# Summing the weighted values of every second early pair on TensorE instead of VectorE

## The reference

```python
q = x @ Wq + bq
kv = (x @ Wdown + bdown) @ Wup + bup
k, v = split(kv.reshape(B, T, 16, 16), 2, axis=-1)     # 16 heads of 8 each
att = softmax(einsum('bthd,btgd->bthg', q, k) / sqrt(8), axis=-1)   # g: 16 heads of the same token
out = einsum('bthg,btgd->bthd', att, v).reshape(B, T, 128) @ Wout + bout
...
x = x + attention(xn) + experts0(xn)       # 8 experts, 2 per token
x = x + long_convolution(xn) + experts1(xn)
```

## Time and profile before

| | |
|---|---|
| three runs | 1330.55, 1329.0, 1339.67 us; median 1330.55 |
| the profiled execution | 1335.22 us, of which 1333.3 us are the span of the trace |
| busy in the span | PE 1042.1, PEld 879.2, DVE 739.9, ACT 583.7, POOL 803.9 us |
| DVE in L1187, all 32 pairs | 141.0 us, 4406 ns each |
| PE in L838 (sums of scores), 11 pairs | 105.4 us, 767 ns a record |

### The profile page before, as it was taken

How to read it: one execution, slowest core, us unless ns; L and a number is a source line. 1 busy time by engine, 2 the same in 40 slices (tenths; PEclk the granted TensorE clock), 3 DMA queues, 4 the chain that set the end, 5 groups by cost and what they waited for, 6 DMA issues and landing times. The chain is left out here.

```text
span 1333.3 us, 19064 instructions
## 1 busy us (share of the span) xinstructions
PE 1042.1 (78%) x6498; PEld 879.2 (66%) x6498; DVE 739.9 (55%) x953; ACT 583.7 (44%) x1518; POOL 803.9 (60%) x669
## 2 busy tenths in 40 slices
PE   5553776788988898888714678898879999999995
PEld 4521333367777777777613577888868888888884
DVE  7755988998888898888697643211122200000007
ACT  1200111166676777767503673000006666666651
POOL 4065675568888888888875136566544544444444
PEclk9876886799999999999856888998979999999998
DMA  9912322335554555555281021698966867666649
GB/s 294 355 47 102 120 84 109 108 93 151 155 162 139 154 170 149 161 150 159 68 325 57 1 84 44 197 279 252 296 196 195 270 193 196 194 190 196 199 135 356
DMA packets 120245, 226.03 MB, mean 170 GB/s; under 512 B 16961, under 2 KB 80405, under 8 KB 118102
## 3 DMA queue, kind: packets, MB, share of 16 engines
q1 hardware_dynamic: 102164, 188.45, 46.1%
q0 software_dynamic: 17600, 35.71, 7.3%
q10 hardware_dynamic: 386, 0.66, 0.2%
HBM read 157.33 MB, written 67.42 MB: 169 GB/s over the span
## 5 line engine op out<-in xcount | busy, mean ns | idle before, releaser
L498 POOL DMA_INDIRECT y_tok<-FF,yidx x284 | 283.3, 997 | 205.9 <-ACT FF L586 142.6
L490 POOL DMA_INDIRECT sorted_x<-XN,idx x256 | 247.9, 968 | 140.1 <-issue 88.0
L810 PE MATMUL ps<-FF 128*128 128x128 f32 x2272 | 285.8, 280 | 0.0
L810 PEld LDWEIGHTS ps<-FF 128*128 128x128 f32 x2272 | 274.0, 197 | 15.6 <-issue 4.8
L797 PE MATMUL ps<-FF 128*128 128x256 f32 x1136 | 272.3, 383 | 0.0
L576 ACT ACTIVATE FF<-ps,FF 128x256 f32<-128x256 f32 x568 | 231.4, 473 | 36.8 <-PE ps L797 29.1
L797 PEld LDWEIGHTS ps<-FF 128*128 128x128 f32 x1136 | 206.9, 192 | 22.7
L294 POOL TENSOR_TENSOR BG<-TPB 128x2048 f32<-128x2048 f32 x42 | 188.8, 4519 | 30.0 <-ACT TPB L603 20.8
L838 PE MATMUL ps<-BG,cst 128*128 128x512 f32 x176 | 105.4, 767 | 57.8 <-DVE BG L1144 40.5
L1176 DVE TENSOR_TENSOR BG<-ps,TPB 128x1024 f32<-128x1024 f32 x128 | 147.3, 1212 | 0.0
L1187 DVE TENSOR_REDUCE BG<-BG 128x256 f32<-128x4096 f32 x32 | 141.0, 4406 | 0.0
(11 more groups left out here) (203 smaller groups left out, 1462.0 us busy)
## 6 DMA issues: line engine op xcount, KB each, us to landing
FF<-in_moe SPq DMA_DIRECT2D x142, 514.0 KB
TPB<-in_kpad SPq DMA_DIRECT2D x22, 1024.0 KB
sorted_x<-TPB SPq DMA_DIRECT2D x36, 520.0 KB, 5.4
FF<-sorted_x SPq DMA_DIRECT2D x142, 130.0 KB
BG<-y_tok SPq DMA_DIRECT2D x12, 1024.0 KB, 9.2
FF<-in_kpad SPq DMA_DIRECT2D x10, 1024.0 KB
y_tok<-FF,yidx POOLq DMA_INDIRECT x284
xt_d<-BG SPq DMA_DIRECT2D x16, 256.0 KB, 4.4
```

The source lines that it names most:

```text
L490: pool.indirect_dma_start(sorted_x[layer], bass.IndirectOffsetOnAxis(ap=idx[:, k, j:j + 1], axis=0), XN[:, j, :], None).then_inc(s_sc, 16)
L498: pool.indirect_dma_start(y_d[layer], bass.IndirectOffsetOnAxis(ap=yidx[:, G % 4, r:r + 1], axis=0), ys[:, G % 4, r * D:(r + 1) * D], None ...
L810: t = pe.matmul(psY[:, r * P:(r + 1) * P], hT[:, G % 2, m, r * P:(r + 1) * P], wc[:, G % 4, HID + m * D:HID + (m + 1) * D], start=False, s ...
```

## The change

For the pairs 0, 2, 4, 6 and 8 (`BY_PE`) the sum over the 16 products moves from DVE to PE. The layout follows: ACT writes those values with the head ahead of the channel, and the weights with the query's head innermost; DVE's four products are written as 16 slices of 256 (tile, channel, query head); PE adds the slices by 16 matmuls with the identity into `psH[1]`, at the start of its step m+2 (`sum_values`); DVE scales them from PSUM in its step m+2, between `scores` and `weighted` (`by_sums`). As `psH[1]` is needed for that, the queries of all early pairs lie in `psH[0]`: `evac_qkv(m)` waits for the product of pair m-1, where it waited for that of pair m-2, and the evacuation of pair 1 moves behind the exponential of the routing. PE's step 10 waits, ahead of its first expert tile, for the scaling of pair 8.

```diff
+BY_PE = (0, 2, 4, 6, 8)
...
 def evac_qkv(m, t):
                 if m < OWN:
                     if t == 0:
-                        wait(act, s_own, m - 1)
-                    for dst, c in ((psH[m % 2][:, t * D:(t + 1) * D], 0), (qkv[:, m % 4, t, D:2 * D], D)):
+                        wait(act, s_own, m)
+                    for dst, c in ((psH[0][:, t * D:(t + 1) * D], 0), (qkv[:, m % 4, t, D:2 * D], D)):
...
-                    act.copy(qkv[:, m % 4, t, 2 * D:3 * D], bank[:, 2 * D:3 * D]).then_inc(s_qkv, 1)
+                    v, w = qkv[:, m % 4, t, 2 * D:3 * D], bank[:, 2 * D:3 * D]
+                    if m in BY_PE:
+                        v, w = v.rearrange("p (g e) -> p g e", e=DH), w.rearrange("p (e g) -> p g e", e=DH)
+                    act.copy(v, w).then_inc(s_qkv, 1)
...
 def pair_exp(b):
-                act.activation(psP[:, :], S[:, b % 2, :], ACT.Exp, scale=SCALE).then_inc(s_exp, 1)
+                if b in BY_PE:
+                    w = psP[:, :].rearrange("p (t g h) -> p t h g", t=2, g=H)
+                else:
+                    w = psP[:, :].rearrange("p (t h g) -> p t h g", t=2, g=H)
+                act.activation(w, S[:, b % 2, :].rearrange("p (t h g) -> p t h g", t=2, g=H), ACT.Exp, scale=SCALE)\
+                    .then_inc(s_exp, 1)
...
-            for m in range(2):
-                for t in range(2):
-                    evac_qkv(m, t)
+            for t in range(2):
+                evac_qkv(0, t)
             act.wait_ge(s_rin, 1)
             act.activation(best[:, 4, :], best[:, 4, :], ACT.Exp).then_inc(s_ex, 1)
+            for t in range(2):
+                evac_qkv(1, t)
...
+            def sum_values(m):
+                pe.wait_ge(s_pv, m + 1)
+                wait(pe, s_on, m - 1)
+                for g in range(H):
+                    t = pe.matmul(psH[1][:, 0:2 * D], ident, prodv[:, g * 2 * D:(g + 1) * 2 * D],
+                                  start=(g == 0), stop=(g == H - 1))
+                t.then_inc(s_vs, 1)
...
             for b in range(LAST_STEP + 1):
                 tiles = tiles_of(b)
+                if b - 2 in BY_PE:
+                    sum_values(b - 2)
                 if b == T_FIRST:
                     pe.wait_ge(s_qkv, 2 * QKV_APART)
+                    pe.wait_ge(s_on, BY_PE[-1] + 1)
                     rows_X(0, 0)
...
 def weighted(b):
-                summed = mark(dve.tensor_reduce(Sm, psP[:, :].rearrange("p (n g) -> p n g", g=H), AX.X, ALU.add))
+                if b in BY_PE:
+                    w = psP[:, :].rearrange("p (t g h) -> p t h g", t=2, g=H)
+                else:
+                    w = psP[:, :].rearrange("p (t h g) -> p t h g", t=2, g=H)
+                summed = mark(dve.tensor_reduce(Sm.rearrange("p (t h) -> p t h", t=2), w, AX.X, ALU.add))
+                by_pe = b in BY_PE
+                for t in range(2 if by_pe else 0):
+                    v = qkv[:, b % 4, t, 2 * D:3 * D].rearrange("p (g e) -> p g e", g=H)
+                    for g0 in (0, H // 2):
+                        n, so = H // 2, t * 256 + g0 * H
+                        w = psP[:, so:so + n * H].rearrange("p (g h) -> p g h", g=n)
+                        i = dve.tensor_tensor(
+                            prodv.rearrange("p (g n) -> p g n", g=H)[:, g0:g0 + n, t * D:(t + 1) * D]
+                            .rearrange("p g (e h) -> p g e h", e=DH),
+                            w[:, :, None, :].to_broadcast([P, n, DH, H]),
+                            v[:, g0:g0 + n, :, None].to_broadcast([P, n, DH, H]), ALU.mult)
...
                 if b >= 2:
                     add_heads(b - 2)
+                if by_pe:
+                    dve.wait_ge(s_v, inverted)
+                    return
                 dve.wait_ge(s_pv, b + 1)
                 reduced = mark(dve.tensor_reduce(O, prodv.rearrange("p (n g) -> p n g", g=H), AX.X, ALU.add))
                 dve.wait_ge(s_v, max(inverted, reduced))
+                by_sums(b, O.rearrange("p (t h e) -> p t h e", t=2, e=DH))
...
                 if b < NPAIR:
                     scores(b)
+                if b - 2 in BY_PE:
+                    dve.wait_ge(s_vs, BY_PE.index(b - 2) + 1)
+                    by_sums(b - 2, psH[1][:, 0:2 * D].rearrange("p (t e h) -> p t h e", t=2, e=DH))
                 if b >= 1:
                     weighted(b - 1)
```

More of the change, by code:

```diff
@@ L237, in mixed_layers @@
         s_S = sem("scores_psum")
+        s_vs = sem("values_psum")
         s_sub = sem("scores_ready")
@@ L1140, in own_product @@
                     for e0 in (0, n):
-                        q = psH[b % 2][:, t * D + e0 * H:t * D + (e0 + n) * H].rearrange("p (e h) -> p e h", e=n)
+                        q = psH[0][:, t * D + e0 * H:t * D + (e0 + n) * H].rearrange("p (e h) -> p e h", e=n)
                         k = qkv[:, b % 4, t, D + e0 * H:D + (e0 + n) * H].rearrange("p (e g) -> p e g", e=n)
@@ L1170, in weighted @@
                 dve.wait_ge(s_exp, b + 1)
-                summed = mark(dve.tensor_reduce(Sm, psP[:, :].rearrange("p (n g) -> p n g", g=H), AX.X, ALU.add))
-                for t in range(2):
+                if b in BY_PE:
[14 more added lines that the diff above has]
+                            v[:, g0:g0 + n, :, None].to_broadcast([P, n, DH, H]), ALU.mult)
+                for t in range(0 if by_pe else 2):
                     v = qkv[:, b % 4, t, 2 * D:3 * D].rearrange("p (e g) -> p e g", e=DH)
@@ L1175, in weighted @@
                         n, o, so = H // 2, t * 2048 + h0 * D, t * 256 + h0 * H
+                        w = psP[:, so:so + n * H].rearrange("p (h g) -> p h g", h=n)
                         i = dve.tensor_tensor(
                             prodv[:, o:o + n * D].rearrange("p (h e g) -> p h e g", h=n, e=DH),
-                            psP[:, so:so + n * H].rearrange("p (h g) -> p h g", h=n)[:, :, None, :]
-                            .to_broadcast([P, n, DH, H]),
+                            w[:, :, None, :].to_broadcast([P, n, DH, H]),
                             v[:, None, :, :].to_broadcast([P, n, DH, H]), ALU.mult)
@@ L1188, in weighted, with by_sums @@
                 dve.wait_ge(s_v, max(inverted, reduced))
+                by_sums(b, O.rearrange("p (t h e) -> p t h e", t=2, e=DH))
+            def by_sums(b, o):
                 wait(dve, s_ot, b - 2)
-                dve.tensor_tensor(On[:, b % 3, :].rearrange("p (n e) -> p n e", e=DH), O.rearrange("p (n e) -> p n e", e=DH),
-                                  Rc[:, :, None].to_broadcast([P, 2 * H, DH]), ALU.mult).then_inc(s_on, 1)
+                dve.tensor_tensor(On[:, b % 3, :].rearrange("p (t h e) -> p t h e", t=2, e=DH), o,
+                                  Rc.rearrange("p (t h) -> p t h", t=2)[:, :, :, None].to_broadcast([P, 2, H, DH]), ALU.mult)                    .then_inc(s_on, 1)
             def combine(i):
```

## The result

Before, the median was 1329.4 us over 20 runs beside the changed kernel; after, 1338.5 us. The ratio is 1.0059 with a 95% interval of 1.004 to 1.0078: 7.8 us more (5.3 to 10.4), where +8.1 was forecast. The profiled execution after (1328.67 us) is the shortest of its runs and the one before (1335.22) is above its median, so the two are compared by stage, each from its own first product of DVE (75.59 us before, 74.30 after).

What follows compares the result with a forecast made beforehand. The early steps were taken as bound by a 16.96 us loop over PE with cold sums, DVE's work just inside it. Terms of 3.4 + 4.7 = +8.1 us on the median 1330.55 gave 1338.7 us, range 1318 to 1349.

Steps and rivals of the forecast that it cites:

- Odd steps gain nothing: Odd early steps 3 to 9: DVE loses 4.8 us of work but waits that much longer for PE; gain 0.
- The loop over PE: Early steps: DVE's product, PE's sums of scores and qkv, ACT's copy, next product; 16.96 us, just longer than DVE's 16.39.
- The new sums are warm: Even steps: PE's 32 added records run at full clock in 6.92 us, the following sums of scores in 6.86 us.
- Even steps, +0.3 us: Even early steps: DVE waits 0.31 us for PE's sums, scales in 0.43 us, takes its next product 0.3 us later.
- Steps 2 and 6, +1.4 us each: The two early steps that begin behind a pause: 0 to 2.8 us late each, the middle taken.
- the lower bound: Steps 2 and 6: PE takes up its new sums during the pause, so they cost nothing, 0 us.
- the rival of one more pause: PE's program gets 320 records longer and one more pause comes, 6.9 us, giving 1345.6 us; chance 0.12.
- +3.4 was forecast: Lateness from the early steps ahead of step 10: 0.3 + 0.3 + 1.4 + 1.4 = 3.4 us.
- The argument that pauses lie at a qkv tile: Against the rival that the pauses go (1317.8 us, chance 0.07): both lie at a qkv tile, which the change leaves alone.
- Step 10, +4.7 us: First expert tile waits for PE's 6.92 us of sums and 0.53 us of scaling: 278.20 for 273.50, +4.7 us.
- The edits at nothing: Single bank of queries, later evacuation of pair 1 and strided access, all taken as covered by waits or idle time: 0 us.
- Nothing explains the pauses: Said in the rival that the pauses of 14.42 and 7.48 us go: at most 20.9 us gained, 1317.8 us; chance 0.07.

Runs made afterwards that it cites:

- e1_no_pair8: The changed kernel, but DVE sums pair 8 itself, so the first expert tile waits for no new sums; ratio to the kernel before 1.0044 (1.0016 to 1.0072).
- the kernel held back: The changed kernel with POOL's scatter held until DVE's fourth product, then run without a pace; ratio to the kernel before 1.0837, +111.4 us.

## Why the prediction came out right

- **Odd steps gain nothing.** Shown from three sides: DVE's relief alone is worth +0.8 us (-3.3 to +4.9); without pauses, odd steps are 17.14, 17.14 and 16.76 us, with sums of about 10 us that start at half clock; with PE's gap filled the sums take 7.03 and the step falls to 14.78. The loop over PE is the bound. (The profile after has one odd step without a pause, step 7, of 16.09 us, 0.96 less than before: its sums took 9.07 us for 10.09.)
- **The new sums are warm.** 7.07 us, for 6.92 forecast, and the sums of scores behind them 7.03 to 7.13, for 6.86, where no pause lies between; behind a pause, in steps 2 and 8, they took 8.83 and 9.19. In the kernel with runs of six the granted clock is 1.00 through both. The Trainium skill, "TensorE: Matmul & The Clock Gate", section "HAM oscillation — how this bites in real kernels", has it that contiguous work is not throttled back, and work between waits is; these windows agree, for the first half by the 1.00 of the even step, for the second by the 0.50 with which the sums behind the gap of the odd step begin.
- **Even steps, +0.3 us.** Mis-sized: -0.3 in the profile after in steps 4 and 6, as the sums were out before DVE asked for them (the pauses ahead of these steps gave PE the time); step 8, with a pause, took 6.48 more. Without pauses they are 16.66, 16.98, 17.76 and 16.99 us, about as before.
- **Steps 2 and 6, +1.4 us each.** The size was right by accident. PE did its sums inside the first pause (from 112.52 to 130.00, in pieces), so step 2 cost nothing (the lower bound), and step 6 nothing either; what made the last product 3.73 us late is that the pauses moved: step 8 is 6.48 us longer, step 3 3.51 longer, step 5 4.33 shorter. That is the rival of one more pause, in part: it was priced at 6.9 us on top of the terms, and here another pause shrank and other steps were 2 us shorter. So that the early steps came to +3.7 where +3.4 was forecast is luck. The argument that pauses lie at a qkv tile, which the change leaves alone, failed in step 8, where the pause lies at the new sums and the transposes.
- **Step 10, +4.7 us.** Measured 4.35, and without the last pair the tile stands 15.8 us behind the last product. This term is more than half of the 8.08 us at the tile; on the whole time its share is not shown, as e1_no_pair8 is not told apart from the changed kernel.
- **The edits at nothing** cost +0.7 us (-3.3 to +4.8).
- **"Nothing explains the pauses"** was the blank of the prediction. That they hang on the pace of POOL's scatter is shown: with waits after every six transfers they go, without a pace news comes up to 88 us late. That they grow with PE's number of records is likely by the kernels with runs of 12, but there the single bank came with the records. By this, moving work to PE beside such a run can have a price that none of the rows read before showed.

## What to carry to other kernels

Moving 4.4 us from an engine that waits in every step buys nothing; find the loop that ends last, and the gap in it that costs the clock. An unexplained wait in the trace of before is part of the sum: try what else runs in it before adding work to the engine that it holds. Here breaking POOL's runs was worth 8 us (3.5 to 12.8) to the old kernel, while the change lost 8 (5.3 to 10.4).

## What was not expected of the hardware

A long unbroken run of POOL's indirect transfers (1.27 us apart) slows PE and holds up the news from it: run through without a pace, they spread six of PE's records over 13 us and let ACT take up PE's transposes 88 us late; with runs of six there was no pause at all; with runs of 12 there was one of 7.9 us in the kernel before, and three with waits of 17 to 23 us with PE's additional records. What the two share is not settled. Late instructions don't show as the cause: in the kernel held back, no transfer of the queues that the profile calls "instruction" falls between 136 and 299 us, and PE stopped and went on inside that time. Nor is it settled whether the length of a run counts or the gap behind it, as the broken runs also waited for their rows to land.
